# NF4 weights decoded by a chain of eight Prelus and one VectorE operation a unit

## The reference

```python
Q = einsum('btx,dx->btd', layernorm(x), Wq) + bq
K = einsum('bpx,dx->bpd', ctx, Wk) + bk
x = x + einsum('btp,bpd->btd', softmax(Q K^T / 32), ctx)
w = NF4_CODE[q].reshape(-1, 64) * absmax[:, None]   # for gate, up (3584 x 1024) and down (1024 x 3584)
g, u = einsum('bsh,mh->bsm', layernorm(x), Wg), einsum('bsh,mh->bsm', layernorm(x), Wu)
out = x + einsum('bsm,hm->bsh', silu(g) * u, Wd)
```

## Time and profile before

| | |
|---|---|
| median of 3 runs | 1909.53 us (1909.39 to 1909.66) |
| profiled execution, first to last instruction | 1907.6 us |
| instructions | 29498 |
| PE (TensorE matmul) | 1895.8 us, 99% |
| DVE (VectorE) | 1666.6 us, 87% |
| ACT (ScalarE) | 1362.3 us, 71% |
| POOL (GpSimd) | 586.0 us, 31% |
| DMA | 326.14 MB, mean 171 GB/s |
| granted TensorE clock | 1.000 over the span |

### The profile page before, as it was taken

One profiled execution on the slowest core, in us unless ns is written; L12 is line 12 of the kernel. 1 busy time (PEld: TensorE's weight loads), 2 busy tenths in 40 slices (PEclk: granted clock), 3 DMA queues, 4 the chain that ended last, 5 costly groups with the idle time before them and its releaser, 6 DMA issues.

```text
span 1907.6 us, 29498 instructions
## 1 busy us (share of the span) xinstructions
PE 1895.8 (99%) x9758; PEld 963.5 (51%) x9758; DVE 1666.6 (87%) x2652; ACT 1362.3 (71%) x2503; POOL 586.0 (31%) x804
## 2 busy tenths in 40 slices
PE   9999999999999999999999999999999999999999
PEld 4487888744444444444444444444444444444444
DVE  7978999869899999999998898999999899996963
ACT  3887776687787887887887977977989999900000
POOL 2023343302333333333332332332445333301110
PEclk9999999999999999999999999999999999999999
DMA  9338999954564554554554454455669998964462
GB/s 357 71 84 187 262 263 281 297 170 122 117 160 122 128 149 127 123 148 123 121 145 132 114 148 127 118 147 144 145 176 233 239 236 213 259 243 138 150 237 83
DMA packets 437640, 326.14 MB, mean 171 GB/s; under 512 B 371680, under 2 KB 371952, under 8 KB 435568
## 3 DMA queue, kind: packets, MB, share of 16 engines
q1 hardware_dynamic: 393280, 170.55, 39.1%
q0 software_dynamic: 44032, 153.65, 24.4%
q10 hardware_dynamic: 176, 0.07, 0.0%
HBM read 154.31 MB, written 82.31 MB: 124 GB/s over the span
## 4 chain that ended last, share of the span: by engine, by line
PE 83%; ACT 5%; DVE 5%; issue 2%; SPq 0%; DMA 0%; DVEq 0%; POOL 0%; ACTq 0%
PE ps L2346 46%; PE ps L2389 26%; PE ps L1710 7%; PE ps L1678 2%; ACT sq L364 2%; PE ps L1745 2%; ACT sq L360 1%; DVE w L380 1%; PE ps L1649 0%; DVE halves L451 0%; DVE T L1154 0%; SPq L1543 0%; DVE tail L2496 0%; PE ps L1422 0%; ACT tail L2420 0%
## 5 line engine op out<-in xcount | busy, mean ns | idle before, releaser
L2346 PE MATMUL ps<-T,wS 128*128 128x512 f16 x4704 | 1017.2, 379 | 2.1 <-DVE T L1437 1.2
L2346 PEld LDWEIGHTS ps<-T,wS 128*128 128x128 f16 x4704 | 459.7, 98 | 556.5 <-issue 4.0
L364 ACT ACTIVATE sq<-sq 128x512 f32<-128x512 f32 x898 | 507.7, 619 | 0.0
L380 DVE SCALAR_TENSOR_TENSOR w<-sq,w 128x512 f32<-128x512 f32 x590 | 441.0, 748 | 51.8 <-ACT sq L364 41.2
L360 ACT ACTIVATE sq<-q 128x512 f32<-128x512 int32 x560 | 339.3, 626 | 134.7 <-DVE w L380 133.1
L2389 PE MATMUL ps<-T,tail 128*128 128x512 f16 x1584 | 344.8, 379 | 0.9 <-DVE tail L2544 0.6
L442 POOL CAST halves<-w 128x512 f16<-128x512 f32 x215 | 203.2, 967 | 283.8 <-DVE w L380 153.6
L2389 PEld LDWEIGHTS ps<-T,tail 128*128 128x128 f16 x1584 | 154.8, 98 | 188.3 <-issue 1.0
L2282 POOL DMA_DIRECT2D keep_h<-tail x196 | 106.2, 542 | 246.6 <-DVE tail L2496 244.4
L451 DVE SCALAR_TENSOR_TENSOR halves<-w,halves 128x512 f16<-128x512 f32 x240 | 165.1, 697 | 6.3 <-POOL halves L442 5.5
L2389 PE MATMUL ps<-T,wS 128*128 128x512 f16 x768 | 168.4, 379 | 0.0
(11 more groups left out here) (245 smaller groups left out, 1869.9 us busy)
## 6 DMA issues: line engine op xcount, KB each, us to landing
keep_h<-tail POOLq DMA_DIRECT2D x196, 256.0 KB, 2.4
tail<-keep_h POOLq DMA_DIRECT2D x66, 512.0 KB, 4.4
wS<-keep_h POOLq DMA_DIRECT2D x32, 512.0 KB, 4.4
T<-in_x SPq DMA_DIRECT2D x13, 1024.0 KB, 8.3
q<-in_L_ffn_up_q POOLq DMA_DIRECT2D x52, 256.0 KB, 3.1
q<-in_L_ffn_gate_q POOLq DMA_DIRECT2D x48, 256.0 KB, 3.1
q<-in_L_ffn_down_q POOLq DMA_DIRECT2D x42, 256.0 KB, 4.3
keep_x<-T SPq DMA_DIRECT2D x38, 256.0 KB, 4.3
```

Source lines behind the costliest of these rows:

```text
L364: nc.scalar.activation(place, place, ACT.Square, bias=b, scale=a).then_inc(un.s_act, 1)
L380: nc.vector.scalar_tensor_tensor(out=out, in0=square_place(un, u, i - 1), scalar=FACTORS[i - 1][1], in1=un.w[:, buf, :], op0=ALU.add, op1= ...
L2346: last = nc.tensor.matmul(ps[:, bank, :], un.wS[:, z % SLOTS, a, kt, :], t.Tp[side][product][:, :, b, kt, :], start=fresh and n == 0, stop ...
```

## The change

A unit's value is now made by eight Prelu activations on ScalarE, one after another in place, from the codes: each computes y = scale * x + bias and multiplies y by alpha where it is negative. Then one VectorE operation adds a constant and multiplies by the block's factor. A unit holds one buffer of `sq` from its first Prelu to that operation. The ScalarE order interleaves two units. The codes' buffer is free after a unit's first Prelu (before: after its last square and its first VectorE operation).

```diff
+BENDS = [(0.09105003625154495, -0.11252861469984055, 2.3341853618621826), (1.0, -0.19289961457252502, 1.3058918714523315),
...
+ZERO_BENT = 0.15385550260543823
+OPS = len(BENDS)
...
-CREDIT, FULL, FIRST_DOWN = (9, 14), (35, 50), CH_PAIRS
+CREDIT, FULL = (6, 12), (30, 42)
...
+BEND_ORDER = sorted(((u, i) for u in range(GATE_UP_UNITS + DOWN_UNITS) for i in range(OPS)), key=lambda n: OPS * n[0] + 2 * n[1] + n[0] % 2)
...
     if used is not None:
-        queue.wait_ge(un.s_act, OPS * (used + 1))
-        queue.wait_ge(un.s_fac, STEPS * used + 1)
+        queue.wait_ge(un.s_act, BEND_COUNT[used, 0])
...
+def bend(nc, act, un, u, i):
+
+    place, (scale, bias, alpha) = bend_place(un, u), BENDS[i]
     if i == 0:
         act.wait_ge(*loaded_at(un, u))
...
+        wait(act, un.s_fac, u - SQ_RING + 1)
+        nc.scalar.activation(place, un.codes[code_slot(u)], ACT.Prelu, bias=bias, scale=scale, alpha=alpha).then_inc(un.s_act, 1)
+    else:
+
+        act.wait_ge(un.s_act, BEND_COUNT[u, i - 1])
+        nc.scalar.activation(place, place, ACT.Prelu, bias=bias, scale=scale, alpha=alpha).then_inc(un.s_act, 1)
...
+def scaled_unit(nc, dve, un, t, u):
+
+    chunk, mat, half, buf = unit_place(u)
+    dve.wait_ge(un.s_act, BEND_COUNT[u, OPS - 1])
...
+    nc.vector.scalar_tensor_tensor(out=out.rearrange("p (b j) -> p b j", j=QBLOCK),
+                                   in0=bend_place(un, u).rearrange("p (b j) -> p b j", j=QBLOCK), scalar=-ZERO_BENT,
                                    in1=s, op0=ALU.add, op1=ALU.mult).then_inc(un.s_fac, 1)
```

VectorE's order of a gate or up stage becomes: unit 0, low parts of the stage before (pieces 1 and 2), unit 1, low parts (pieces 3 to 6), unit 2, the low part of piece 0, two sums, unit 3, two sums. Before, a stage's pieces 1 and 2 were made within the stage itself. On ScalarE the early high parts (pieces 0 to 20) are placed by a table:

```diff
+    due = {(0, 2): z - 6, (0, 3): z - 5, (1, 2): z - 4, (1, 3): z - 3, (1, 4): z - 2, (1, 5): z - 1, (2, 1): z}.get((u % 4, i), -1)
...
 def decode_act(nc, act, un, t):
 
...
+    for u, i in BEND_ORDER:
+        yield bend(nc, act, un, u, i)
```

The quotas of attention and of slots 0 to 10 stay. The others change, and GpSimd's casts of the down part go to the phases that the plan gives them (before: six at the end of the slots, the others each behind a code load):

```diff
-        steps = (2 * (4 * STEPS + 4 + PIECES), 2 * 4 * OPS)
+        steps = (2 * (4 + 4 + PIECES), 2 * 4 * OPS)
...
-            return self.dealt[k] if k in self.dealt else ((2 if k // SPLIT_STEPS % 2 or k % 2 else 3), 6)
-        return 8, 9 if phase - DOWN_PHASE < FIRST_DOWN else 10
+            return self.dealt[k] if k in self.dealt else (2, 5)
+        return 4, 9
...
-                    used = code_before(u)
-                    if used is not None and used >= GATE_UP_UNITS + SEAM_CASTS:
-                        piece_hi_pool(nc, pool, un, t, GATE_UP_PIECES + used - GATE_UP_UNITS)
+
+        def casts_due(phase):
+            for z in PLAN.casts.get(phase, ()):
+                piece_hi_pool(nc, pool, un, t, z)
...
-            loads_due(DOWN_PHASE + m + Q_AHEAD)
+            if m > 0:
+                loads_due(DOWN_PHASE + m + 1)
+                casts_due(DOWN_PHASE + m + 1)
...
-                streams.dve.run(DOWN_PHASE + m, STEPS + 1 if c == CH_PAIRS - 2 and group in LEFT_BEHIND else 0)
+                streams.dve.run(DOWN_PHASE + m, 2 if c == CH_PAIRS - 2 and group in LEFT_BEHIND else 0)
```

More of the change, by code:

```diff
@@ L346, in square, with bend_place @@
[L346 to L350, removed]
+def bend_place(un, u):
+    return un.sq[:, u % SQ_RING, :]
+def bend(nc, act, un, u, i):
+    place, (scale, bias, alpha) = bend_place(un, u), BENDS[i]
     if i == 0:
         act.wait_ge(*loaded_at(un, u))
[L353 to L357, removed]
-        else:
-            wait(act, un.s_fac, STEPS * used[0] + used[1] + 2)
-        nc.scalar.activation(place, un.codes[code_slot(u)], ACT.Square, bias=b, scale=a).then_inc(un.s_act, 1)
-    else:
-        act.wait_ge(un.s_act, OPS * u + SQUARES.index((f, level - 1)) + 1)
-        nc.scalar.activation(place, place, ACT.Square, bias=b, scale=a).then_inc(un.s_act, 1)
@@ L569, in __init__ @@
                 dif[v] = d
-            act_unit(GATE_UP_UNITS + v, {4: (z,)} if v and not high_on_pool(z) else {})
+        a = 0
+        for u, i in BEND_ORDER:
+            a += 1
+            bent[u, i] = a
+            for z in high_after((u, i)):
+                a += 1
+                hi[z] = a
+            z = GATE_UP_PIECES + u - GATE_UP_UNITS - 1
+            if i == 4 and u > GATE_UP_UNITS and not high_on_pool(z):
+                a += 1
+                hi[z] = a
         z = GATE_UP_PIECES + DOWN_UNITS - 1
@@ L581, in __init__ @@
                 self.of_act[n] = hi[z]
-        for (u, i), n in sq.items():
-            f, level = SQUARES[i]
-            if level == 0 and u > 0:
-                used = square_used(u, f)
-                self.of_dve[n] = fac[used[0], used[1] + 1] if used else lo[GATE_UP_PIECES - 1]
+        for (u, i), n in bent.items():
+            if i == 0 and u >= SQ_RING:
+                self.of_dve[n] = fac[u - SQ_RING]
         for z, n in hi.items():
@@ L632, in __init__ @@
                     if d in at_cast:
-                        self.casts.setdefault(min(phase, DOWN_PHASE - 1), []).extend(at_cast[d])
+                        self.casts.setdefault(phase, []).extend(at_cast[d])
                     if d in at_lo:
@@ L637, in __init__ @@
             self.act.append(a)
-            while loaded < GATE_UP_UNITS + DOWN_UNITS and self.codes_free(loaded, sq, fac, a, d):
+            while loaded < GATE_UP_UNITS + DOWN_UNITS and self.codes_free(loaded, bent, fac, a, d):
                 self.loads.setdefault(phase + 1, []).append(loaded)
@@ L2305, in gpsimd @@
             loads_due(HIDDEN_PHASE + k)
-            for z in PLAN.casts.get(HIDDEN_PHASE + k, ()):
-                piece_hi_pool(nc, pool, un, t, z)
+            casts_due(HIDDEN_PHASE + k)
             if k in H_AT:
```

219 lines of the change are left out of this document (76 added, 143 removed).

## The result

The changed kernel takes 1946.33 us (median of 4 runs, 1937.50 to 1957.71); the kernel before, run beside it, 1909.46. The ratio is 1.0195, with a 95% interval of 1.0159 to 1.0231: slower by about 2%, where 1906.4 was forecast. The profiled execution took 1945.68 us, with a span of 1943.9.

What follows compares the result with a forecast made beforehand. The prediction took TensorE, busy 1895.8 of 1907.6 us, as the bound. Span 1907.6 - 3.8 us of returned waits + 0.7 of new ones = 1904.5, plus 1.9 outside it: 1906.4 us, range 1904.0 to 1912.5.

Steps and rivals of the forecast that it cites:

- What goes and what comes: Decode: 672 fewer VectorE operations (503.9 us) and 336 fewer on ScalarE (173 us), worth at most 5.1 us.
- what a Prelu costs: Decode on ScalarE: a Prelu takes the square's time, 619 ns long, 0.47 to 0.57 us from start to start.
- E: Prelu and Silu don't share a table, so table loads ring the gate stages' Silus: 1957; chance 0.04.
- F: A Prelu of 0.58 us or more from start to start makes TensorE wait for a copy: 1912 or above; chance 0.03.
- D: Gate and up products: ten weight pieces turned only 3 slots ahead come late, +10 us, 1916; chance 0.08.
- Where each wait goes: TensorE's waits beside decode work, at 160, 395 to 399, 592, 1399 and 1613 us, shrink by 3.8 us in sum.
- 0.7 us for waits that the new deal makes: Whole kernel: new waits from the changed order of work cost 0.7 us against the 3.8 us gained.
- What tightens, (3): Down product: codes and transposes come some 15% faster with DMA engines 0.98 busy; pieces 7 to 13 steps ahead cover any landing.
- What tightens, (4): GpSimd's casts move to their own phase, with h loads behind; a cast is about 1 us, cover 25 us.
- Where each wait goes, the attention phases: Attention: VectorE's steps in phases 10 to 19 fall from 13 to 7; the wait at 160.7 loses 0.8 of 1.16 us.
- Rival C: The waits only change hands, for instance ScalarE 1 us later in phases 0 to 9: 1909; chance 0.12.
- The ceiling: Seven TensorE waits beside decode work, 5.1 us or 0.27% of the time, are the most a lighter decode can return.

Runs made afterwards that it cites:

- e_pace: Changed kernel with the down product's decode quota cut to one unit a step, from nine in eight steps; 1927.64 us, ratio 1.0108.
- c_turns_full: c_turns with ScalarE's quota in the last 28 slots cut from 42 to 36 in ten slots; 1907.14 us, ratio 0.9979.
- c_fixed: Changed kernel with e_ring, e_seam and the turn of piece 8 at slot 7 together; 1936.29 us, ratio 1.0122.
- e_downcast: Changed kernel with GpSimd's casts put ahead of the code loads of the same step in the down product; 1943.29 us, ratio 1.0185.
- e_ahead: Changed kernel with the down product's code loads issued early again, those of step m+3 behind step m; 1940.72 us, ratio 1.0158.
- e_seam: Changed kernel with GpSimd's casts put ahead of the code loads inside the slots; 1936.81 us, ratio 1.0153.
- e_ring: Changed kernel with the high parts of pieces 6 and 7 later in ScalarE's attention order, which also moves piece 8's turn; 1931.16 us, ratio 1.0111.
- c_turns: c_fixed with one decoded unit a down step, and pieces 3 to 8 turned in the phases of the kernel before; 1909.94 us, ratio 0.9995.
- e_turn8: Changed kernel with only the transposing DMA of piece 8 moved back to slot 7 from phase 77; 1937.69 us, ratio 1.0145.
- b_pace: Kernel before with its down quota raised to 11 units in ten steps, from one a step; 1940.73 us, ratio 1.0153.

## Why the prediction was wrong

- **What goes and what comes, what a Prelu costs: right.** 672 and 336 operations fewer, L358 786 ns, a Prelu 620 ns, two table loads. Rivals E and F are out, and D too: no wait for a turned piece in the long middle. VectorE's total fell by 444 us and not by 504. Of the 60 us some 18 are operations that got longer (L382 820 ns, 741 before; L416 737, 697 before). For the rest, operations of 0.69 us start 0.61 us apart (1563.64, 1564.25), so that the removed ones covered less than the sum of their lengths; how much of it that is wasn't measured.
- **Where each wait goes: right, and hidden by what is new.** By the start of the n-th matmul the changed kernel gains 0.45 us at 160 (forecast 0.8), 2.0 at 395 to 399 (1.5), 0.36 at 592 (0.3) and 0.53 at 1399 (0.5). At 1613 it loses 6.4, but e_pace and c_turns_full gain 0.72 there (0.7). That makes 4.1 in all, where the sum had 3.8.
- **The sum's term that failed: 0.7 us for waits that the new deal makes.** It had no working behind it. In the trace the new waits and the clock behind them are some 40 us: 36.3 lost in the whole, with 3.3 returned. The next three points say which steps left them out.
- **What tightens, (3): failed.** "Pieces are 7 to 13 steps ahead, which covers any landing time seen" looked at the wrong thing. In the changed kernel's trace no matmul waited for a piece; VectorE waited, for a cast and for a last Prelu, in program order ahead of the evictions. (c_fixed's 6.1 us show that a piece can be late as well.) I had read codes and transposes "some 15% faster" off the plan as if engines at 0.98 could deliver that. The decode ended in step 43 (its last L416 at 1653.85) and not at 40, though TensorE itself had stood still on the way, and the cost was 11.5 us in this trace. e_pace removes it, e_downcast doesn't, e_ahead only moves it.
- **What tightens, (4): failed.** I counted a cast at 1 us and asked who stands behind the cast. What mattered was what stands ahead of it, five code loads at 4 us each, and that VectorE waits for it and ScalarE for VectorE: 6.9 us, of which e_seam removes 5.4.
- **Where each wait goes, the attention phases: failed by omission.** It counted VectorE's and ScalarE's decode steps and left out SyncE's transposes. That the plan now turned pieces 1 and 2 nine phases later, and piece 8 ten phases earlier, inside the batch, follows from the changed plan. It cost 6.2 us in the attention and about 4 of the 11.5 at the late loads, shown by e_ring with c_turns and by e_turn8.
- **The clock was in no term.** 10.6 of the 36.3 us are matmuls at the lower granted clock. It fell five times, each time in or behind one of the waits at the late loads, the seam and the two ends of groups. The new waits should have carried it.
- **Rival C** (waits change hands, 1909) had the mechanism and a small part of its size: it allowed for waits as small as those removed.
- **The ceiling held.** No version gains more than the 5.1 us that it allows. c_turns_full's median lies 3.1 us under that of the kernel before on the same chip (1907.14 and 1910.26), its trace 2.3. That the first is just what the sum promised is luck in part: the kernel before had medians from 1909.46 to 1910.26 in these series.

## What to carry to other kernels

When a change shortens work that a plan deals out, the plan's new dates are part of the change: list for each queue what moved ahead of what, above all loads ahead of casts and transposes among other transposes, and price each with the landing times under load. Don't let a lighter engine set a faster pace than the transfers beside it can keep; a decode that asks for more than its supply makes the in-order engine wait in front of the evictions. Count a new wait of TensorE as possibly more than its length, for the clock behind it (3.3 us became 5.1). In e_ahead the clock fell behind waits of 1.97, 2.29 and 2.44 us too, and not behind one of 2.69, so these traces give no length from which on it does. And before a loss in one trace is explained, look at the same place in the other traces: 9.6 us here were mostly chance.

## What was not expected of the hardware

- More room for GpSimd's descriptors made all transfers slower: code loads 4.1 to 11.1 us, transposes 6.0 to 15.1 us, 230 to 193 GB/s.
- One transposing DMA among others took 19.3 us to land (361.50), and its neighbour 10.21 us to issue. In the kernel before, from 404 to 700 us, such a transpose takes 3.4 us to land and 1.3 to issue.
- A wait of 3.3 us was followed by 5 us at a mean granted clock of 0.66.
- Times that vary more where there are waits, but not by a rule: 20 us over four runs of the changed kernel and 4 us over eleven of c_turns_full, yet 3 us over four runs of b_pace, which loses 32.7 us. What a trace shows at one such place (9.6 us at 360 to 372) is a sample.
